# Two edge stages of a graph kernel: message stores and the edge-weight fetch move from SyncE's queue to ScalarE's

## The reference, cut to what matters

```
# layer 0, "gated edges"
z   = concat([h[dst], h[src], edge_attr])                # 192 wide
m   = sigmoid(z @ W_f + b_f) * softplus(z @ W_s + b_s)
m   = m * exp(-distance**2 / 18)
out = segment_sum(m, dst) + h
# layer 1, "plain edges"
x   = concat([h[src], h[dst], e])                        # e is edge_weight1, one number an edge
m   = relu(x @ W1 + b1) @ W2 + b2
out = segment_sum(m, dst)
```

## Time and profile before

| | us |
|---|---|
| median of 3 runs | 5973.34 (5969.6 to 5974.13) |
| profiled execution, its own time | 5968.36 |
| its span | 5966.2 |
| gated edges, 293 to 1018 | 725 |
| plain edges, 1223 to 1875 | 652 |

### The profile page before, as it was taken

The page is one execution under the profiler, slowest core; times in us unless marked ns, Lnnn a source line. Parts: engine busy times, 40 slices in busy tenths (PEclk is TensorE's granted clock), DMA queues, the critical chain, the costliest instruction groups (busy, mean ns, idle before and its releaser), DMA issues. The chain is left out here.

```text
span 5966.2 us, 125979 instructions
## 1 busy us (share of the span) xinstructions
PE 4223.1 (71%) x31967; PEld 3151.4 (53%) x31967; DVE 3287.5 (55%) x7378; ACT 2956.2 (50%) x7228; POOL 3281.1 (55%) x3335
## 2 busy tenths in 40 slices
PE   1078887568885299995798759999499893155564
PEld 0067776546664166663575336666267552155452
DVE  3844444856666633334787953333578799512156
ACT  0256665634445544443684224444278325544447
POOL 0955553356652355551786975555078687666620
PEclk6599999879997699997899989999799996576675
DMA  9455554845544744443233444444233335522224
GB/s 239 89 125 126 126 127 102 168 83 100 102 101 106 193 111 115 117 116 72 60 84 76 101 110 112 116 117 117 58 73 83 81 92 107 112 45 45 46 57 135
DMA packets 1392327, 618.38 MB, mean 104 GB/s; under 512 B 876801, under 2 KB 1351357, under 8 KB 1390426
## 3 DMA queue, kind: packets, MB, share of 16 engines
q1 hardware_dynamic: 1307692, 534.90, 38.0%
q0 software_dynamic: 63360, 65.01, 6.4%
q10 hardware_dynamic: 21140, 17.02, 1.0%
HBM read 379.93 MB, written 236.09 MB: 103 GB/s over the span
## 5 line engine op out<-in xcount | busy, mean ns | idle before, releaser
L934 ACT ACTIVATE hot_e<-iota_n,rel 128x256 f32<-128x256 f32 x980 | 423.0, 499 | 629.8 <-DMA m_r<-m_d 283.5
L974 DVE TENSOR_TENSOR acc<-acc,part_e 128x128 f32 x1176 | 336.3, 286 | 622.1 <-DMA hn_a<-g_d 272.4
L1969 ACT ACTIVATE leak_l<-tp_l,bcat 128x512 f32<-128x512 f32 x588 | 364.9, 685 | 600.4 <-issue 426.0
L1994 DVE COPY zT_l<-zTp_l 128x512 f32<-128x512 f32 x196 | 135.6, 692 | 950.6 <-DMA g_d<-gout_a 327.2
L957 PE MATMUL part_e<-z_e,hot_e 128*128 128x128 f32 x1568 | 308.2, 373 | 438.5 <-DVE acc L974 243.1
L1060 POOL DMA_INDIRECT z_l<-h_d,src_i x392 | 391.2, 998 | 312.0 <-PE zTp_l L1101 217.0
L1060 POOL DMA_INDIRECT z_l<-g_d,src_i x392 | 390.4, 996 | 310.5 <-PE zTp_l L1101 215.6
L1060 POOL DMA_INDIRECT z_e<-h_d,src_i x392 | 378.4, 965 | 314.5 <-PE zTp_e L1101 215.7
L957 PEld LDWEIGHTS part_e<-z_e,hot_e 128*128 128x128 f32 x1568 | 281.7, 277 | 465.0 <-DVE acc L974 253.5
L1196 POOL DMA_INDIRECT z_e<-h_d,row_of_e x392 | 385.8, 984 | 247.7 <-PE uTp_e L1536 102.1
L957 PE MATMUL part_e<-m_e,hot_e 128*128 128x128 f32 x3136 | 426.5, 288 | 122.2 <-DVE acc L974 65.1
(11 more groups left out here) (419 smaller groups left out, 11144.1 us busy)
## 6 DMA issues: line engine op xcount, KB each, us to landing
m_d<-m_m SPq DMA_DIRECT2D x196, 138.0 KB
h_d<-h SPq DMA_DIRECT2D x56, 448.0 KB
relb_e<-rel_d SPq DMA_DIRECT2D x196, 128.0 KB
near_e<-h_d SPq DMA_DIRECT2D x392, 64.0 KB
near_e<-g_d SPq DMA_DIRECT2D x392, 64.0 KB
relb_l<-rel_d SPq DMA_DIRECT2D x196, 128.0 KB
near_l<-h_d SPq DMA_DIRECT2D x392, 64.0 KB
z_l<-rest_d SPq DMA_DIRECT2D x196, 128.0 KB
```

Source lines behind the costliest of these rows:

```text
L934: ins = self.nc.scalar.activation(self.hots[k][:, t, :], self.S["iota_n"][:, :], ACT.Abs, scale=-1.0, bias=self.S["rel"][:, ds(n * BLK + t ...
L974: ins = self.nc.vector.tensor_tensor(x, x, part[:, t % 2, :, 0:x.shape[2]], ALU.add)
L1969: nc.scalar.activation(leak[u % 2][:, q, :], tp[q][:, :], ACT.Relu, bias=bcat[:, 0, q:q + 1], scale=1.0 - SLOPE).then_inc(leak_ready, 1)
```

## The change

In both stages SP's loop keeps only loads. In the gated stage the store of a block's messages goes to ACT, which begins the store of block n - 3 at the end of its body for block n. In the plain stage ACT begins the fetch of `aux` for block n + 3 at the start of its body for block n, and the store of block n - 2 at its end, behind the ReLU; the last waits for the stores to land move with them. The transfers themselves, their sizes and their rings are the same. ACT's loops for the plain stage end one turn earlier and the last four blocks stand alone, since the last block's weights are fetched in two pieces.

```diff
# gated_edges, SyncE
-                def store(n, u):
-                    sp.wait_ge(m_ready, n + 1)
-                    sp.dma_start(m_rows[ds(n, 1)].rearrange("g p b c -> (g p) b c")[:, :, 0:C], m[u % RINGS][:, :, 0:C]).then_inc(m_out[u % RINGS], 16)
...
                     for u in range(LEAD, LEAD + UN):
                         load(i * UN + u, u)
-                        store(i * UN + u - LATE, u - LATE)
# gated_edges, ScalarE
+                def store(n, u):
+                    act.wait_ge(m_ready, n + 1)
+                    act.dma_start(m_rows[ds(n, 1)].rearrange("g p b c -> (g p) b c")[:, :, 0:C], m[u % RINGS][:, :, 0:C]).then_inc(m_out[u % RINGS], 16)
...
                     if has(n, 1):
                         gates(n - 1, u + 1)
                         sums.hot(act, n - 1, (u + 1) % 2)
+                    if has(n, 3):
+                        store(n - 3, u + 1)
# plain_edges, SyncE
-                def load(n, u):
-                    k = u % RINGS
-                    near.load(sp, n, u)
-                    sp.dma_start(aux[k][:, :, :], ew_rows[ds(n, 1)].rearrange("n r h e -> (n h) r e")).then_inc(aux_in[k], 32)
...
-                        store(i * UN + u - LATE, u - LATE)
+                blocks(sp, lambda n, u, i: near.load(sp, n, u))
# plain_edges, ScalarE
+                def fetch(n, u):
+                    k = u % RINGS
+                    need(act, z_used, n - RINGS + 1)
...
+                        act.dma_start(aux[k][:, :, :], ew_rows[ds(n, 1)].rearrange("n r h e -> (n h) r e")).then_inc(aux_in[k], 32)
+
                 def body(n, u, i):
                     k = u % 2
+                    if not (isinstance(n, int) and n + 3 >= NB):
+                        fetch(n + 3, u + 3)
                     if has(n, 1):
                         sums.hot(act, n - 1, 1 - k)
                     act.wait_ge(z_used, n + 1)
                     need(act, mp_ready, n - 1)
                     nc.scalar.activation(uT[k][:, :], uTp[k][:, 0:2 * P], ACT.Relu, bias=S["b1"][:, 0:1]).then_inc(uT_ready, 1)
+                    if has(n, 2):
+                        store(n - 2, u + 2)
```

More of the change, by code:

```diff
@@ L1299, in _ @@
                     load(n, n)
-                    if n >= LATE:
-                        store(n - LATE, n - LATE)
                 with sp.Fori(0, (NB - LEAD) // UN - 1) as i:
@@ L1394, in _ @@
                 sums.hot(act, NB - 1, 1)
+                for n in range(NB - 3, NB):
+                    store(n, n)
+                for k in range(RINGS):
+                    act.wait_ge(m_out[k], 16 * len(range(k, NB, RINGS)))
             @block.vector
@@ L1483, in _ @@
             def _(sp):
-                ew = io["edge_weight1"].rearrange("n a -> a n")
-                ew_rows = ew[0, 0:(NB - 1) * BLK * P].rearrange("(n r h e) -> n r h e", r=2, h=2, e=P)
-                def load(n, u):
-                    k = u % RINGS
-                    near.load(sp, n, u)
-                    sp.dma_start(aux[k][:, :, :], ew_rows[ds(n, 1)].rearrange("n r h e -> (n h) r e")).then_inc(aux_in[k], 32)
[L1492 to L1500, removed]
-                near.store_far(sp)
[L1503 to L1510, removed]
-                        store(i * UN + u - LATE, u - LATE)
[L1512 to L1518, removed]
+                near.store_far(sp)
+                blocks(sp, lambda n, u, i: near.load(sp, n, u))
             @block.tensor
@@ L1576, in _, with store @@
             def _(act):
+                ew = io["edge_weight1"].rearrange("n a -> a n")
+                ew_rows = ew[0, 0:(NB - 1) * BLK * P].rearrange("(n r h e) -> n r h e", r=2, h=2, e=P)
+                def store(n, u):
+                    act.wait_ge(m_ready, n + 1)
+                    act.dma_start(m_rows[ds(n, 1)].rearrange("g p b c -> (g p) b c")[:, :, 0:WIDTH], m[u % RINGS][:, :, 0:WIDTH]).then_inc(m_out[u % RINGS], 16)
+                def fetch(n, u):
+                    k = u % RINGS
+                    need(act, z_used, n - RINGS + 1)
+                    if isinstance(n, int) and n == NB - 1:
+                        r0 = n * BLK * P
+                        act.dma_start(aux[k][:, 0, :], io["edge_weight1"][r0:r0 + 2 * P, :].rearrange("(h e) a -> h (e a)", h=2)).then_inc(aux_in[k], 16)
+                        act.dma_start(aux[k][0:1, 1, 0:LAST_E - 2 * P], ew[:, r0 + 2 * P:E]).then_inc(aux_in[k], 16)
+                    else:
+                        act.dma_start(aux[k][:, :, :], ew_rows[ds(n, 1)].rearrange("n r h e -> (n h) r e")).then_inc(aux_in[k], 32)
                 def body(n, u, i):
                     k = u % 2
+                    if not (isinstance(n, int) and n + 3 >= NB):
+                        fetch(n + 3, u + 3)
                     if has(n, 1):
@@ L1583, in body @@
                     nc.scalar.activation(uT[k][:, :], uTp[k][:, 0:2 * P], ACT.Relu, bias=S["b1"][:, 0:1]).then_inc(uT_ready, 1)
-                blocks(act, body)
+                    if has(n, 2):
+                        store(n - 2, u + 2)
+                act.wait_ge(s_blank, 1)
+                for n in range(3):
+                    fetch(n, n)
+                for n in range(LEAD):
+                    body(n, n, 0)
+                with act.Fori(0, (NB - LEAD) // UN - 1) as i:
+                    for u in range(LEAD, LEAD + UN):
+                        body(i * UN + u, u, i)
+                for n in range(NB - UN, NB):
+                    body(n, n, 0)
                 sums.hot(act, NB - 1, 1)
+                for n in range(NB - 2, NB):
+                    store(n, n)
+                for k in range(RINGS):
+                    act.wait_ge(m_out[k], 16 * len(range(k, NB, RINGS)))
             @block.vector
```

## The result

The changed kernel takes 5917.9 us (median of 4 runs) against 5971.5 for the kernel before on the same chip: ratio 0.9912, 95% interval 0.9896 to 0.9928, so 54 us less. The forecast was 121 us less. The measured time lies in the range and the sign is right, but the gain is less than half of the forecast. The profiled execution has a span of 5914.6 us (before 5966.2).

The account below looks back on a forecast made before the run. SP's queue was taken to bound both stages; 39 us gated, 79 plain and 3 at the stages' ends made 121 us off 5973, so 5852. The range was 5770 to 5930.

Parts of the forecast that it names:

- SP sets the pace in both stages: Both stages: SP's back-to-back instructions hold PE at 7.29 us a gated block and 6.56 us a plain one.
- a queue that never waits: SP's queue, both stages: no row shows its loads waiting, so it never catches up and sets its own pace.
- Gated step: Gated stage: the message store leaves SP, 0.40 us a block after the discount, 98 blocks, 39 us.
- rival 2: Gated stage bound by VectorE's own chain: a few us there at most, plain stage 50 to 80; 5890 to 5923; chance 0.22.
- discount of 1.49: Both stages: SP slows 0.49 us per us a block shortens, so shedding s us of its work gains s / 1.49.
- So the pace can't fall below 5.0: Plain stage: POOL's four gathers need 5.0 us a block, PE's turns 4.96, so at most 1.56 us can be gained.
- 0.81 us a block, 79 us: Plain stage: store and `aux` leave SP, worth 0.81 us a block after the discount, 98 blocks, 79 us.
- 0.81 us a transfer: SP's queue: mean step of a gated block, 7.29 / 9; plain 0.82; lower bound 0.4 us.
- rival 3: POOL's gather delays all queues, so no gain, 5965 to 5980; sign: SP's 0.7 us instructions more often; chance 0.07.
- ScalarE's cost, nothing: ACT, both stages: added transfers of 0.5 us each fit its waits, 2.4 us cover gated and 1.8 plain.
- rival 4: ACT's transfers beside the gather get SP's slow spells: plain block 7.4 us, 82 us more, 6055; chance 0.09.
- Rival 1: Both stages: SP leaves the path, PE's own pace is left; 179 to 210 us less, 5763 to 5794; chance 0.15.

## Why the prediction was wrong in size

**SP sets the pace in both stages: right, but not all of the way, and the sign for it was missed.** Each half gave its gain alone, and the waits of `hotT` for `relb` are gone. The prediction wanted waits in SP's loads of hundreds of us in both stages; they came to 42.7 us in the plain one and 1.2 us in the gated one. So "a queue that never waits" was no proof by itself: in the changed gated stage SP's queue hardly ever waits either, and `relb` is in time.

**Gated step, 39 us: right.** 36 us alone, 33 us between the two traces, 6.80 us a block for 6.89. How it came about is less sure. `hotT` no longer waits for `relb`, so this fetch of SP's doesn't hold the block; PE does still wait for VectorE's sums (changed kernel, 340 to 920), as in rival 2, though for less than the 57.5 us of the earlier trace rows:

```profile
PEld part_e L957 <- DVE acc L974: 49.5, 66, 1.9
PE part_e L957 <- DVE acc L974: 35.7, 32, 1.6
```

That 6.80 also contains late signals is likely from the 5.85 of the quick conditions, but not shown. So the discount of 1.49, which gave the right size, stays unproved, and that the size came out is in part luck. Rival 2, with a gated stage that gives a few us at most, falls by the 36 us.

**"So the pace can't fall below 5.0", plain stage: the step that failed.** 5.0 us is what GpSimd needs for its gathers and 4.95 what TensorE needs, each by itself. Beside the gathers, in the case's conditions, the two don't fit together: the floor is 6.27 us. The 4 x 1.25 counts 0.30 us ahead of every gather, but the first of a block waits for `z_used`, and that signal comes late: over the plain stage the four gathers take 4.94 us and the pause ahead of the next block 1.36 us (medians), 6.3 in all. In the kernel before they are 4.86 and 1.41, so the pause was there to be read. SP stood only 0.29 us above this floor, not 1.56. The term was put at 0.81 us a block, 79 us, and measured at 17 us in the traces (0.29 us a block in the steady stretch, less at the stage's start) and 22 us by itself. That is about 60 of the 67 us by which the forecast missed; the 3 us at the ends and the rest of the gated term are the others. The two turns 4.96 us apart in the earlier trace rows were a block that followed a late one, whose turn had begun 9.89 us earlier, at 1490.23:

```profile
1490.23 0.38 PE L1527 MATMUL uTp_e<-ident,z_e 128*128 128x128 f32 x2
1492.30 1.22 PE L1530 MATMUL uTp_e<-aux_e,w1t 2*128 2x256 f32 x2 [1.69 <-DMA aux_e<-in_edge_weight_dram]
...
1492.50:1499.00 6.50, 6.50 (x33) 4.93 (x34) 3.12 (x14) 3.12 (x6) 3.63 (x4) 0.50 0.64 106
```

One pair shows what PE can do, not what the stage can keep up. The rows show a second price of the late `aux` too: after the wait of 1.69 us TensorE's granted clock was 0.50, its 1.2 GHz level, for the rest of that block. Over the steady stretch it was 0.92 before and is 1.00 now. So the rise that the prediction thought its highest case might need did come, and the gain stayed small, since the floor is not TensorE's own work: in 1480 to 1520 of the kernel before, 281 matmuls make blocks of 6.26 us at a granted clock of 0.91. How much of the 22 us came by the clock was not separated.

The trace of before had the floor in it. Its window 1290 to 1350, early in the plain stage, and its waits there:

```profile
1290.00:1350.00 60.00, 52.94 (x433) 41.34 (x434) 42.02 (x186) 30.38 (x59) 38.43 (x40) 1.00 0.46 92
...
ACT hot_e L934 <- DMA m_r<-m_d: 23.3, 8, 4.5
...
PEld part_e L957 <- issue: 10.0, 18, 1.2
```

Here `relb` was never waited for, and a block took 60 / (433 / 44) = 6.10 us, with the same unnamed stops of PE and the same senseless releaser as after the change. That releaser stands in the waits of before over 1300 to 1850, the stretch of the earlier trace rows, as well, in 79 of some 84 blocks:

```profile
ACT hot_e L934 <- DMA m_r<-m_d: 257.5, 79, 5.7
```

I read the early stretch of the gated stage and not this one.

**0.81 us a transfer: right as a mean, wrong as a price.** It is about 0.5 us of issuing and the rest delay beside the gathers. Here rival 3 had most of the mechanism: the gather lays a delay on SP's queue and on signals, and its sign came, slow instructions of SP's more often than before (over 0.6 us 12% of them before, 18% after). L1208 in the changed kernel, for 2/333/714 in the earlier trace rows:

```profile
L1208 SPq DMA_DIRECT2D near_e<-g_d x392: 3/16/765, 1191.0 to 1802.3; - x196
```

Its consequence, no gain, was wrong by the 0.29 us, and the delay is not on all queues, as the next paragraph shows. The Trainium skill ("DMA: Bandwidth & Descriptors", section "Issuing engines are not separate DMA queues") says that starting DMAs from several engines saves only the time to begin them, which is usually small. In the quick conditions the runs agree, 1.000; in the case's the saving is small too but clear, 0.991.

**ScalarE's cost, nothing: right.** 0.42 and 0.26 us for its transfers, hidden before its wait of 3.11 us; rival 4 falls. Its two transfers at 1503.59 and 1504.18 fell into the 3.67 us that SP's four `near` took, and over the whole plain stage no store took ScalarE's queue more than 0.52 us to begin:

```profile
L1547 ACTq DMA_DIRECT2D m_d<-m_e x98: 378/418/520, 1223.3 to 1822.3; - x98
```

Rival 1 falls with the floor.

**The range: held by luck.** The measured 5918 lies in it because it was stretched over rival 2's times, 5890 to 5923. Rival 2 had the two stages the other way round: it gave the gated one nearly nothing and the plain one 50 to 80 us, and they gave 36 and 22.

## What to carry to other kernels

Take the next bound from a stretch of before in which the present bound isn't late, over ten blocks at least, and not from the shortest distance of two events; where a bound is a sum of an engine's instructions, read the pause between two blocks as well as that between two instructions. A queue that never waits is a suspect, not proof: ask whether what it begins comes late. When an idle stretch ends with "issue" or with a transfer that the engine doesn't read, on several engines at the same moment, look for late signals and for what runs beside them; moving work between queues won't lower that floor. And a move off a queue is worth only the distance to that floor: here the first plain transfer bought all of it, the second nothing.

## What the runs showed of the hardware

The same program ran in two conditions 7% apart (5565 and 5970 us), each steady over a whole set. In the slower one, beside GpSimd's indirect gathers, some of SyncE's instructions take 0.7 us, even a MOVE, and a signal of TensorE's arrived 4.2 us late in the block shown. The instructions with which ScalarE begins its transfers stay at 0.24 to 0.52 us in the same plain stage. Halving the plain gathers took the lateness of the signals away there (127 and 142 us) and thinned SyncE's slow instructions from 3.0 and 2.7 a block to 1.4 and 0.9; in the quicker condition gathers of the same number and length did no such harm. What separates the two conditions stays open, and so does the worth of spacing the gathers in the slower one.
